# Unused products in the routing loop of the capacity experts, and at the end of the set-up

## The chip, the cores and the metric

The kernel runs on one core of one Trainium2 chip. The metric is the device time of one execution in microseconds (us), lower is better. Before the change the median of three runs is 2647.92 us (2641.19 to 2651.87).

## The reference

A chain of twelve stages works on `x` of 8 x 512 rows of 128 numbers. The stage that matters here is the feed-forward layer L0, which is used twice, as stage 0 and as stage 2, with the segment attention between them:

```python
x = x + 0.5 * L0_ffn(layernorm(x))      # stage 0
x = x + L0_attn(layernorm(x))           # stage 1
x = x + 0.5 * L0_ffn(layernorm(x))      # stage 2
...                                     # nine more stages

def L0_ffn(x):                          # 8 kinds: 7 experts and one that does nothing
    weights = softmax(x @ router_w.T + router_b)
    vals, idx = top_k(weights, 2)
    # each expert takes the first 512 of the 4096 rows that chose it
    h = relu(inputs[e] @ experts_inter[e])
    out[e] = (h @ experts_out[e]) * weight
    # every row gets back what its experts made of it;
    # the idle kind gives the row itself times its weight
```

## The kernel before, in words

`x` stays in SBUF for the whole kernel, as 32 tiles of 128 rows; four tiles make a block, so there are eight blocks (B = 8, TB = 4). Each stage is a block of instruction streams, one for each engine, tied by semaphores and written out by hand; a barrier of all engines (`clear`) stands between two stages. There is no planner: an engine does its list in the order in which it is written.

**The unused products.** `stir` (L174 to L178) issues n TensorE products of the 128x128 identity in bf16 with itself, repeated to 512 columns, into a PSUM bank whose content nobody reads. The kernel calls it in many places.

**The set-up** (`setup`, L181) loads x and the weights and prepares a few matrices. TensorE does almost nothing in it: two small products for the router and the gate (L249, L252), then, when VectorE has summed the eight adapters (L301, L303), one transpose (L315). VectorE then goes on with the signatures and the last copy (L311), and the barrier follows.

**The routing loop** is the first part of `capacity_experts_ffn` (L776). On TensorE, for b in 0 to 8: `turn_batch(b)` transposes the four tiles of x of block b (L867) into one of two banks in turn; then come two unused products (L919, shown under the line of the helper, L178); then `route(b - 1)` multiplies the turned block b - 1 by the router's eight columns (L874). `turn_batch(b)` waits until ScalarE has copied block b - 2 out of PSUM; `route(b)` waits for the copy of block b. ScalarE copies each turned block (L1094, `copy_xnT`) and, from the third copy on, normalises the four tiles of block b - 2 (L1087). VectorE takes the statistics of the eight blocks (L133, L138, L141), and GpSimd makes the deviations from them (L1139 to L1142). SyncE meanwhile clears two rows of results in HBM (L848).

When all eight blocks are routed, VectorE alone chooses the experts (`choose`, L963 to L977), TensorE counts (L924, L925), sixteen more unused products run, and the rows of each expert are found (`find_slots`, L885), gathered by indirect DMA (L1151), multiplied (L903, L912) and scattered (L1162). The next stage reads them back.

Of the kernel before, what the change touches and what calls it, by code (L numbers as in the profile page):

```python
# [61 lines left out]
def semaphores(nc, names):  # L62

    names = names.split()
    while len(ALL_SEMS.free) < len(names):
        ALL_SEMS.made += 1
        ALL_SEMS.free.append(ALL_SEMS.ctx.enter_context(nc.semaphore(f"stage{ALL_SEMS.made}")))
    taken, ALL_SEMS.free = ALL_SEMS.free[:len(names)], ALL_SEMS.free[len(names):]
    return namedtuple("Semaphores", names)(*taken)  # L70
# [11 lines left out]
def clear(nc, s, last=False):  # L82

    numbers = [h.num for h in s]
    assert not set(numbers) & {h.num for h in ALL_SEMS.free}
    assert min(numbers) > max([h.num for h in ALL_SEMS.lasting], default=-1)
    if last:
        numbers += [h.num for h in ALL_SEMS.lasting]
    nc.all_engine_barrier(sems_to_clear=range(min(numbers), max(numbers) + 1))  # L90
    ALL_SEMS.free = sorted([*s, *ALL_SEMS.free], key=lambda h: h.num)
# [82 lines left out]
def stir(pe, G, bank, n):  # L174

    for _ in range(n):
        pe.matmul(bank, G.ident16[:], G.ident16[:].unsqueeze(1).to_broadcast([P, 4, P]), start=True, stop=True)  # L178

def setup(nc, ctx, inp):  # L181

    sb = lambda n, shape, dt=F32: ctx.enter_context(nc.sbuf_tensor(n, shape, dt))
    G = Shared()

    G.x, G.minus_half = sb("x", [P, NT + TB, D]), sb("minus_half", [P, TB])
    G.ident, G.ident16 = sb("ident", [P, P]), sb("ident16", [P, P], BF16)

    G.WcT, G.bcomb = sb("WcT", [D, D]), sb("bcomb", [P, D])  # L190
    G.M, G.gateT = sb("M", [D, KINDS, D]), sb("gateT", [D, KINDS])
    G.route = sb("route", [D, KINDS + NCT + COMP_H])
    G.table = sb("table", [NCT, T_ALL])
    G.knots, G.inv_temp, G.out_scale = sb("knots", [P, KINDS]), sb("inv_temp", [P, 1]), sb("out_scale", [P, 1])
    G.cb1, G.cw2, G.cb2 = sb("cb1", [COMP_H, 1]), sb("cw2", [COMP_H, 2]), sb("cb2", [P, 2])
    G.half_gamma, G.half_beta, G.desc = sb("half_gamma", [P, D]), sb("half_beta", [P, D]), sb("desc", [P, KINDS])
    with ExitStack() as own:
        s = semaphores(nc, "x_loaded cleared made router_psum router_copied gate_loaded gate_psum gate_copied")
        segment, load_segment, clear_blocks = segment_attention_prepare(nc, ctx, G, inp)
        router, load_router, make_upto, raw_router = capacity_experts_prepare(nc, ctx, own, G, inp)  # L200
        center = own.enter_context(nc.sbuf_tensor("center", [P, P], F32))
        psC = own.enter_context(nc.psum_tensor("psC", [P, 512], F32))
        spline, load_spline, make_order, make_signatures = spline_prepare(nc, own, G, inp)
        adapters, load_weights, load_biases, combine_adapters, turn_adapters, copy_adapters = adapters_prepare(nc, own, G, inp)
        raw_gate = own.enter_context(nc.sbuf_tensor("raw_gate", [D, KINDS], F32))
        with nc.Block() as block:
            @block.sync
            def _(sp):
                for q in range(4):
                    sp.dma_start(G.x[:, q * NT // 4:(q + 1) * NT // 4, :],  # L210
                                  inp["L0_attn_x"].rearrange("b (t p) d -> p (b t) d", p=P)[
                                      :, q * NT // 4:(q + 1) * NT // 4, :]).then_inc(s.x_loaded, 16)
                load_router(sp)
                sp.dma_start(raw_gate[:], inp["L3_ffn_gate_wT"]).then_inc(s.gate_loaded, 16)
                load_biases(sp)
                load_segment(sp)
                sp.wait_ge(s.x_loaded, 64)
                sp.wait_ge(router.router_loaded, 32)

            @block.scalar  # L220
            def _(act):
                load_weights(act)
                load_spline(act)
                act.wait_ge(s.gate_loaded, 16)
                act.wait_ge(segment.seg_loaded, 128)

            @block.gpsimd
            def _(pool):
                pool.memset(G.minus_half[:], -0.5).then_inc(s.cleared, 1)
                pool.memset(G.x[:, NT:, :], 0.0).then_inc(s.cleared, 1)  # L230
                pool.memset(G.ident[:], 0.0).then_inc(s.cleared, 1)
                pool.wait_ge(s.cleared, 3)
                pool.affine_select(out=G.ident[:], in_=G.ident[:], compare_op=ALU.not_equal, fill=1.0,
                                   base=0, pattern=[[-1, P]], channel_multiplier=1).then_inc(s.made, 1)
                pool.wait_ge(s.made, 1)
                pool.tensor_copy(G.ident16[:], G.ident[:]).then_inc(s.made, 1)
                pool.wait_ge(s.made, 2)

                pool.tensor_scalar(center[:], G.ident[:], -1.0 / D, None, ALU.add).then_inc(s.made, 1)
                pool.wait_ge(s.made, 3)  # L240
                make_upto(pool)
                clear_blocks(pool)
                make_order(pool)

            @block.tensor
            def _(pe):
                pe.wait_ge(s.made, 3)
                pe.wait_ge(router.router_loaded, 32)
                pe.matmul(psC[:, 0:KINDS], center[:], raw_router[:], start=True, stop=True).then_inc(s.router_psum, 1)  # L249
                pe.wait_ge(s.gate_loaded, 16)  # L250
                pe.wait_ge(s.router_copied, 1)
                pe.matmul(psC[:, 0:KINDS], center[:], raw_gate[:], start=True, stop=True).then_inc(s.gate_psum, 1)  # L252
                turn_adapters(pe)

            @block.vector
            def _(dve):
                dve.wait_ge(s.router_psum, 1)
                dve.tensor_copy(G.routerT[:], psC[:, 0:KINDS]).then_inc(s.router_copied, 1)
                dve.wait_ge(s.gate_psum, 1)
                dve.tensor_copy(G.gateT[:], psC[:, 0:KINDS]).then_inc(s.gate_copied, 1)  # L260
                combine_adapters(dve)
                make_signatures(dve)
                copy_adapters(dve)
        clear(nc, s + router + segment + spline + adapters)
    return G
# [510 lines left out]
def capacity_experts_ffn(nc, G, inp, tag, rest):  # L776
# [12 lines left out]
    with ExitStack() as ctx:  # L789
# [46 lines left out]
        slots_ps, xT_ps = [pb(f"slots{i}", [P, 512]) for i in range(2)], pb("xT", [D, CAP])  # L836
# [5 lines left out]
        with nc.Block() as block:  # L842
# [19 lines left out]
            def _(pe):  # L862
# [53 lines left out]
                for b in range(B + 1):  # L916
                    if b < B:
                        turn_batch(b)
                    stir(pe, G, slots_ps[0][:], 2)  # L919
                    if b:  # L920
                        route(b - 1)
                pe.wait_ge(s.masked, 1)
# [273 lines left out]
def segment_attention_prepare(nc, ctx, G, inp):  # L1196
    sb = lambda n, shape, dt=F32: ctx.enter_context(nc.sbuf_tensor(n, shape, dt))
    G.seg_w = {n: sb(f"seg_{n}", [D, D]) for n in ("wq", "wk", "wv", "wc")}
    G.seg_bq, G.seg_bk = sb("seg_bq", [D, 1]), sb("seg_bk", [D, 1])
    G.seg_bv, G.seg_bc = sb("seg_bv", [D, 1]), sb("seg_bc", [P, D])  # L1200
    G.seg_P = sb("seg_P", [P, SB, TB, P])
    s = semaphores(nc, "seg_loaded seg_cleared")

    def load(dma):
        for n, w in G.seg_w.items():
            dma.dma_start(w[:], inp[f"L0_attn_{n}T"]).then_inc(s.seg_loaded, 16)
        dma.dma_start(G.seg_bq[:], inp["L0_attn_bq"].rearrange("(d a) -> d a", a=1)).then_inc(s.seg_loaded, 16)
        dma.dma_start(G.seg_bk[:], inp["L0_attn_bk"].rearrange("(d a) -> d a", a=1)).then_inc(s.seg_loaded, 16)
        dma.dma_start(G.seg_bv[:], inp["L0_attn_bv"].rearrange("(d a) -> d a", a=1)).then_inc(s.seg_loaded, 16)
        dma.dma_start(G.seg_bc[:], row_layout(inp["L0_attn_bc"])).then_inc(s.seg_loaded, 16)  # L1210

    def make(pool):
        pool.memset(G.seg_P[:], 0.0).then_inc(s.seg_cleared, 1)
        pool.wait_ge(s.seg_cleared, 1)
    return s, load, make
# [2022 lines left out]
```

## Time and profile before

| | |
|---|---|
| three timed runs, us | 2641.19, 2647.92, 2651.87 |
| the profiled execution, us | 2653.97 |
| its span, first to last instruction, us | 2652.2 |
| mean granted TensorE clock over the span | 0.922 |
| busy share: TensorE, VectorE, ScalarE, GpSimd | 83%, 74%, 67%, 37% |
| instructions in the trace | 47713 |
| stage 0: starts, router's last result read | 34.66, 51.62 us |
| stage 2: starts, router's last result read | 261.2, 288.68 us |

### The profile page before, as it was taken

What the parts mean: (1) busy time and instruction counts of PE and PEld (TensorE: products, weight loads), DVE (VectorE), ACT (ScalarE), POOL (GpSimd) and SP (SyncE); (2) the same over time, 40 slices, a digit from 0 to 9 for tenths busy, and PEclk for the clock granted to TensorE, in tenths of its full rate; (3) what the DMA queues carried; (4) which work ended last, traced back from release to release, by engine and by line L of the source; (5) the groups of instructions that cost most, each with busy time, mean ns of one, the idle gap of its engine ahead of it and who ended that gap; (6) DMA issues with size and microseconds to landing.
All of it is one profiled execution on the core that took longest, in us unless ns stands there. A gap on an engine that the chain in (4) does not pass through costs nothing. (4 is left out here: it accounts for less than half of the span.)

```text
span 2652.2 us, 47713 instructions
## 1 busy us (share of the span) xinstructions
PE 2196.8 (83%) x15155; PEld 1125.9 (42%) x15155; DVE 1958.0 (74%) x5765; ACT 1788.1 (67%) x4541; POOL 988.2 (37%) x1512
## 2 busy tenths in 40 slices
PE   3768785748888888589999999997868888888888
PEld 2446463512222225434444444445334444444453
DVE  4547626759989967768777777776688888888766
ACT  2224223327777774568888878785479999999965
POOL 2643354345445413600000000005645555555437
PEclk8889586759999996799999999999979999999999
DMA  4420514022322310100000000000020111111001
GB/s 140 112 84 13 155 40 135 1 48 59 78 53 55 79 25 1 33 1 1 2 1 1 2 1 2 2 2 1 7 64 1 33 33 33 33 33 33 1 1 32
DMA packets 227640, 94.85 MB, mean 36 GB/s; under 512 B 175746, under 2 KB 215490, under 8 KB 227394
## 3 DMA queue, kind: packets, MB, share of 16 engines
q1 hardware_dynamic: 220864, 83.46, 12.6%
q0 software_dynamic: 3584, 7.58, 1.0%
q8 instruction: 125, 2.05, 0.3%
q10 hardware_dynamic: 2946, 0.77, 0.2%
q14 instruction: 121, 0.99, 0.1%
HBM read 30.66 MB, written 19.17 MB: 19 GB/s over the span
## 5 line engine op out<-in xcount | busy, mean ns | idle before, releaser
L2345 DVE TENSOR_REDUCE s_neg_max<-s_ps_a 128x1 f32<-128x512 f32 x1024 | 662.3, 684 | 141.7 <-PE s_ps_a L2151 129.2
L2613 ACT ACTIVATE s_pT<-s_ps_t 128x512 f32<-128x512 f32 x1024 | 646.1, 659 | 135.8 <-PE s_ps_t L2185 116.4
L2604 ACT ACTIVATE s_first<-s_ps_a,s_neg_max 128x512 f32<-128x512 f32 x512 | 412.0, 805 | 14.0 <-DVE s_neg_max L2345 13.7
L2531 POOL TENSOR_SCALAR s_first<-s_first,s_rec 128x512 f32<-128x512 f32 x384 | 301.6, 801 | 282.6 <-DVE s_rec L2351 282.5
L2197 PE MATMUL s_ps_t<-ident,s_first 128*128 128x128 f32 x2048 | 313.6, 284 | 64.2 <-ACT s_pT L2613 51.2
L2977 DVE CUSTOM_DVE_ANT_0 s_e<-s_ps_a,w_alibi 128x128 f32<-128x128 f32 (+3 forms) x512 | 225.9, 488 | 126.7 <-PE s_ps_a L2813 126.3
L2151 PE MATMUL s_ps_a<-s_lanesT 64*128 64x512 bf16 x1024 | 272.2, 398 | 36.8 <-DMA s_lanesT<-n_lanes 21.2
L2197 PEld LDWEIGHTS s_ps_t<-ident,s_first 128*128 128x128 f32 x2048 | 220.5, 141 | 160.9 <-ACT s_pT L2613 117.4
L2215 PE MATMUL s_ps_o<-s_pT,n_v_pad 128*32 128x512 f32 x2048 | 272.8, 606 | 12.2 <-ACT s_oT L2619 12.2
L3085 ACT ACTIVATE s_e<-s_e,s_neg_max 128x128 f32<-128x128 f32 (+3 forms) x512 | 282.1, 564 | 0.0
L3093 ACT ACTIVATE s_pT<-s_ps_t 128x384 f32<-128x384 f32 (+1 forms) x320 | 156.3, 532 | 115.5 <-PE s_ps_t L2840 88.8
L154 POOL TENSOR_TENSOR s_rstd<-s_ve,minus_half 128x4 f32<-128x4 f32 x24 | 24.7, 1030 | 502.2 <-DVE s_ve L141 501.5
L2185 PE MATMUL s_ps_t<-s_shiftedT,s_lanesT 64*128 64x512 bf16 x512 | 167.2, 385 | 41.1 <-DVE s_neg_max L2345 30.0
L2813 PE MATMUL s_ps_a<-s_k_side,s_q_side 64*128 64x128 f32 (+3 forms) x1024 | 187.1, 460 | 3.6 <-DVE s_neg_max L2977 1.4
L2991 DVE TENSOR_SCALAR s_e<-s_e,s_rec 128x128 f32<-128x128 f32 (+3 forms) x512 | 163.3, 383 | 4.5
L2604 ACT ACTIVATION_READ_ACCUMULATOR s_first<-s_ps_a,s_neg_max 128x1 f32 x512 | 166.2, 325 | 0.0
L2856 PE MATMUL s_ps_vo<-s_pT,s_v 128*64 128x512 f32 (+3 forms) x1024 | 163.3, 441 | 0.0
L2840 PEld LDWEIGHTS s_ps_t<-ident,s_e 64*128 64x128 f32 x2176 | 107.8, 140 | 89.6 <-issue 45.7
L2151 PEld LDWEIGHTS s_ps_a<-s_lanesT 64*128 64x128 bf16 x1024 | 62.1, 93 | 179.1 <-issue 106.3
L2185 PEld LDWEIGHTS s_ps_t<-s_shiftedT,s_lanesT 64*128 64x128 bf16 x512 | 38.5, 93 | 221.2 <-ACT s_pT L2613 160.0
L703 PE MATMUL s_ps_y<-M,s_xT 128*128 128x512 f32 x256 | 119.8, 612 | 10.3 <-DVE x L599 8.3
L2840 PE MATMUL s_ps_t<-ident,s_e 64*128 64x64 f32 x2176 | 115.1, 224 | 13.9 <-issue 4.5
(428 smaller groups left out, 4138.4 us busy)
## 6 DMA issues: line engine op xcount, KB each, us to landing
s_y_rows<-s_zeros SPq DMA_DIRECT2D x4, 2048.0 KB, 10.0
s_parts<-s_y_rows SPq DMA_DIRECT2D x32, 256.0 KB, 3.8
s_token_rows<-s_rows SPq DMA_DIRECT2D x2, 2176.0 KB, 10.3
s_Wi<-L_ffn_experts_inter SPq DMA_DIRECT2D x2, 1792.0 KB
x<-L_attn_x SPq DMA_DIRECT2D x4, 512.0 KB, 8.1
out<-x SPq DMA_DIRECT2D x8, 256.0 KB, 2.3
s_lanesT<-n_lanes SPq DMA_TRANSPOSE x64, 4.6
s_shiftedT<-n_lanes SPq DMA_TRANSPOSE x64, 2.4
```

The lines of the kernel that those rows point to most:

```text
L2151: pe.matmul(sa[n % NA][:], lanesT[rows_of(a), j % 2, 0, pair, t * P:(t + 1) * P], lanesT[rows_of(a), j % 2, 1, pair, :], start=True, stop= ...
L2185: pe.matmul(st[n % NK][:], lanesT[rows_of(a), j % 2, 1, pair, i * P:(i + 1) * P], shiftedT[rows_of(a), p % NS, :], start=True, stop=True). ...
L2197: last = pe.transpose(st[n % NK][:, t * P:(t + 1) * P], first[:, p % NF, 2 * t + a, i * P:(i + 1) * P], G.ident[:])
L2215: last = pe.matmul(o_ps[32 * c:32 * c + 32, :], G.v_pad[j % 2][:, (g % PB * TB + kt) * 2 + c % 2, :], pT[:, (PU * g + 2 * kt + c % 2) % NP ...
L2345: dve.tensor_reduce(neg_max[:, column(n):column(n) + 1], sa[n % NA][:], AX.X, ALU.max, negate=True).then_inc(s.max_ready, 1)
L2531: do.free(pool.tensor_scalar(f, f, rec1[:, n:n + 1], 1.0, ALU.mult, ALU.mult))
L2604: act.activation(first[:, g % NF, n % PU, :], sa[n % NA][:], ACT.Exp, bias=neg_max[:, n:n + 1], accum_out=sum1[:, n % (NR * PU):n % (NR * ...
L2613: act.activation(pT[:, n % NP, :], st[n % NK][:], ACT.Exp).then_inc(s.probs_ready, 1)
L2813: pe.matmul(sa[t % 2][a][:, 0:width(t)], q_side[g % NS][rows, t * P:(t + 1) * P], k_side[g % NS][rows, 0:width(t)], start=True, stop=True) ...
L2840: last = pe.transpose(turn_bank(m, half)[:, first + t * HALF_P:first + (t + 1) * HALF_P], e[rows, g % NF, 2 * t + a, kt * P:(kt + 1) * P], ...
L2977: dve.tensor_tensor_reduce(e[:, g % NF, 2 * t + a, 0:width(t)], sa[t % 2][a][:, 0:width(t)], G.alibi[:, h, (TB - 1 - t) * P:L], -1.0, 3e38 ...
L3085: act.activation(part, part, ACT.Exp, bias=neg_max[:, n:n + 1], scale=-1.0, accum_out=total[:, n:n + 1]).then_inc(s.first_ready, 1)
```

## The change

Two edits. In the routing loop the two unused products stay for blocks 2 to 8 and become five after blocks 0 and 1; the loop runs in stage 0 and in stage 2. At the end of the set-up's TensorE stream ten unused products are added, into the bank psC, whose last content VectorE has taken by then. The wait ahead of them is for the bf16 identity, which GpSimd made at the start of the set-up.

```diff
@@ setup, TensorE
                 pe.matmul(psC[:, 0:KINDS], center[:], raw_gate[:], start=True, stop=True).then_inc(s.gate_psum, 1)
                 turn_adapters(pe)
+                pe.wait_ge(s.made, 2)
+                stir(pe, G, psC[:], 10)
 
@@ capacity_experts_ffn, TensorE
                 for b in range(B + 1):
                     if b < B:
                         turn_batch(b)
-                    stir(pe, G, slots_ps[0][:], 2)
+
+                    stir(pe, G, slots_ps[0][:], 2 if b > 1 else 5)
                     if b:
                         route(b - 1)
```

That is 10 + 2 x 6 = 22 more products of 512 columns, none of which is read.

## Rows read from the trace of the kernel before

**Rows 1.** The page: granted clock in 40 slices of 66.3 us, in tenths.

```profile
PEclk8889586759999996799999999999979999999999
```

**Rows 2.** Busy time by stretch: routing loop of stage 0, its rest, the same of stage 2.

```profile
34.66:51.62 16.96, 16.35 (x114) 13.76 (x114) 10.78 (x73) 14.33 (x33) 13.49 (x32) 1.00 0.67 249
51.62:163.18 111.56, 77.20 (x564) 50.97 (x564) 56.79 (x176) 24.37 (x45) 58.29 (x55) 0.84 0.32 89
261.20:288.68 27.48, 27.37 (x114) 23.40 (x114) 10.75 (x73) 15.51 (x36) 13.48 (x32) 0.50 0.44 164
288.68:405.44 116.76, 83.24 (x564) 53.97 (x564) 56.91 (x176) 21.89 (x40) 58.38 (x55) 0.79 0.30 83
```

**Rows 3.** Order of time, routing loop of stage 0 (start, duration, engine).

```profile
34.66 1.09 PE L867 MATMUL s_ps_xT<-ident,x 128*128 128x128 f32 x4 [5.32 <-PEq L90]
...
35.54 1.06 PE L178 MATMUL s_ps_slots<-ident 128*128 128x512 bf16 x2
...
39.05 0.64 PE L867 MATMUL s_ps_xT<-ident,x 128*128 128x128 f32 x4
...
39.53 0.59 PE L178 MATMUL s_ps_slots<-ident 128*128 128x512 bf16 x2
39.73 0.60 ACT L1094 ACTIVATE s_xnT<-s_ps_xT 128x512 f32<-128x512 f32 x1 [1.64 <-PE s_ps_xT L867]
...
39.96 0.95 PE L874 MATMUL s_ps_up<-routerT,s_xnT 128*128 128x8 f32 x8
...
40.77 0.63 PE L867 MATMUL s_ps_out<-ident,x 128*128 128x128 f32 x4
...
51.62 0.42 DVE L963 TENSOR_TENSOR s_logits<-s_ps_up,s_rstd 128x256 f32<-128x256 f32 x1 [5.64 <-PE s_ps_up L874]
```

**Rows 4.** Order of time, routing loop of stage 2.

```profile
262.10 1.06 PE L178 MATMUL s_ps_slots<-ident 128*128 128x512 bf16 x2
...
262.95 1.06 PE L867 MATMUL s_ps_out<-ident,x 128*128 128x128 f32 x4
...
264.65 1.72 PE L874 MATMUL s_ps_up<-routerT,s_xnT 128*128 128x8 f32 x8
...
266.22 1.09 PE L867 MATMUL s_ps_xT<-ident,x 128*128 128x128 f32 x4
...
269.53 1.09 PE L867 MATMUL s_ps_out<-ident,x 128*128 128x128 f32 x4
...
288.68 0.42 DVE L963 TENSOR_TENSOR s_logits<-s_ps_up,s_rstd 128x256 f32<-128x256 f32 x1 [16.17 <-PE s_ps_up L874]
```

**Rows 5.** Waits in 261:289 (who for whom, us in total, times, longest).

```profile
DVE s_logits L963 <- PE s_ps_up L874: 16.2, 1, 16.2
ACT s_xnT L1094 <- PE s_ps_xT L867: 15.8, 4, 10.7
```

**Rows 6.** Order of time, last part of the set-up.

```profile
28.86 0.48 PE L315 MATMUL psW<-ident,Wsum 128*128 128x128 f32 x1 [12.86 <-DVEq L305]
...
33.48 0.29 DVE L311 TENSOR_SCALAR WcT<-psW 128x128 f32<-128x128 f32 x1
```

**Rows 7.** Granted clock by stretch around the ends of work (columns as in rows 2).

```profile
52.00:56.00 4.00, 0.00 (x0) 0.00 (x0) 3.28 (x9) 3.41 (x9) 0.00 (x0) 0.51 0.15 48
...
255.00:260.00 5.00, 3.23 (x18) 2.71 (x17) 1.61 (x3) 0.00 (x0) 0.00 (x0) 0.82 0.00 0
260.00:265.00 5.00, 3.79 (x15) 2.86 (x15) 3.69 (x24) 1.20 (x2) 2.46 (x5) 0.53 0.42 150
```

**Rows 8.** By stretch after the loop: to the first gather; first to last scatter; both stages.

```profile
51.62:76.35 24.73, 10.12 (x88) 5.15 (x88) 20.93 (x58) 3.79 (x10) 0.00 (x0) 0.65 0.62 178
...
103.03:163.18 60.15, 46.94 (x315) 33.83 (x313) 17.58 (x61) 15.61 (x27) 39.11 (x39) 0.96 0.15 43
288.68:313.32 24.64, 11.01 (x88) 5.33 (x88) 20.88 (x57) 1.95 (x5) 0.00 (x0) 0.64 0.59 164
...
340.19:405.44 65.25, 50.69 (x308) 36.04 (x304) 17.50 (x61) 14.97 (x27) 39.01 (x39) 0.88 0.14 40
```

## The prediction

> **What bounds the kernel now.** I read the page's clock row first: the granted TensorE clock is near full almost everywhere, but the slice from 265 to 331 us shows 5 tenths, and that is where stage 2 begins [rows 1]. Then the busy times by stretch, with both routing loops cut out. The same 114 products take 16.96 us in stage 0 and 27.48 us in stage 2, at a granted clock of 0.50 in the second [rows 2]. So the two loops, which are one piece of code, differ by 10.5 us, and the reader is to see that the slow one is TensorE's: it is busy 27.37 of 27.48 us, and the longest waits there are VectorE's for the last router product (16.2 us) and ScalarE's for a turned block (15.8 us in four waits) [rows 5].
>
> The order of time gives each loop's pace. In stage 2 block 2 is turned at 266.22 and block 3 at 269.53: 3.31 us a block, all of it TensorE at 1.2 GHz [rows 4]. In stage 0 the unused products at 35.54 take 1.06 us a pair, those at 39.53 only 0.59: the clock rose between, after four unused products and eight transposes (the clock column shows 1.00 for the whole loop [rows 2], but the durations before 38.4 are those of 1.2 GHz, so I go by the durations) [rows 3]. From then on TensorE needs 40.77 - 39.05 = 1.72 us a block [rows 3], and ScalarE sets the pace: from its copy of block 2 at 39.73 to the last router product read at 51.62 are 11.89 us [rows 3], six blocks at about 2.0. That tail is what a loop costs once its clock is up; with the clock down it is 21 us. Nothing else covers these microseconds: `choose`, which starts when the loop ends, is VectorE alone, and 24.73 and 24.64 us pass from there to the first gather in the two stages [rows 8]. So what the loop of stage 2 wins moves on into the stage.
>
> **The change, part by part.** Prices in a row of products, from starts. At 1.2 GHz: an unused pair 262.95 - 262.10 = 0.85, so 0.425 for one; a block's router products 266.22 - 264.65 = 1.57; its transposes 3.31 - 0.85 - 1.57 = 0.89 [rows 4]. At 2.4 GHz: transposes 0.48, pair 0.43 (0.215 for one), router products 0.81 [rows 3].
>
> (1) Stage 2's loop. The first product follows the first transposes at 262.10, as before. Five at 1.2 GHz end at 262.10 + 2.13 = 264.23, the transposes of block 1 at 265.1, five more at 267.2. Up to there TensorE has streamed 128 or 512 columns without a pause, against one pair in 3.3 us before. In stage 0 the rise came after 3.7 us of a thinner mix [rows 3], so I take the clock as up when the ten are through, 267.2. Then router products of block 0 (0.81), transposes of block 2 from 268.0, ScalarE's copy 0.68 later as in stage 0 (39.05 to 39.73 [rows 3]), at 268.7, and 11.89 more: 280.6 instead of 288.68, **-8.1**. Bounds: were the clock up at 264.9, 3.7 us after the loop's start, the second five end at 266.2 and the loop at 279.6 (-9.1); if it rises one block later, the router products of block 0 and the transposes of block 2 still cost 1.57 and 0.89: 281.5 or so (-7.2).
>
> That it then stays up I read from stage 0: the same six blocks with two products each run at 1.00 until the loop is over, and the clock is down at 52 us [rows 2, 7]. The Trainium skill speaks against that: "TensorE: Matmul & The Clock Gate", section Part 4: PE-mode transpose, holds that transposes do not count as work for the full clock. By it the two products of a later block stand nearly alone and the clock falls again: term (1) would be about 0 instead of -8.1, which is rival C. The loop of stage 0, half of whose streamed columns are transposes, does not bear it out.
>
> (2) Stage 0's loop. It was up early already. If the clock starts low as before: 34.66, first five from 35.54 to 37.67, transposes to 38.5, where it rose before; the second five at 0.215 to 39.6, router 40.4, copy of block 2 at 41.1 against 39.73: **+1.4**. If the set-up's products leave it up from the first transpose: 34.66 + 0.48 + 1.08 + 0.48 + 1.08 + 0.81 + 0.68 = 39.3: -0.5. I take +1.4, since the clock did fall around the short pause before stage 2: 0.82 in 255:260, 0.53 in 260:265 [rows 7], and the set-up also ends in a pause of about 1 us.
>
> (3) The ten products of the set-up. They start after the transpose, near 29.3, and need 4.27 us at 1.2 GHz: to 33.6. VectorE's last copy ends at 33.77, and the loop starts at 34.66, TensorE having waited 5.32 us [rows 3, 6]. So VectorE's chain hides them: **0**. Without that cover they would be 4.3; as it is 0.1 at most, if the barrier sees their end a little after VectorE's. Nothing queues behind them on TensorE but the barrier; no engine waits for psC.
>
> (4) What follows. The first scatter to the last takes 60.15 us at a clock of 0.96 in stage 0 and 65.25 at 0.88 in stage 2 [rows 8]: the same work, 5.1 apart by where the clock happened to fall. Moving stage 2 by 8 us deals these cards anew. I put 0 in the sum and 5 each way in the range.
>
> Sum against the execution profiled (2653.97 us, of which the span is 2652.2): -8.1 + 1.4 + 0 = -6.7, so 2647.3. That execution lies 6.05 above the median of the runs. The spread of all four, 12.8 us, is about what one loop costs at the low clock (10.5), so some of the runs may have had it up. Taking the whole -6.7 off the median gives 2641.2, taking the median's lower time for a partly warm loop gives 2647.3; I choose the middle, **2644 us**, -0.15%.
>
> **Rivals.**
> (A) The forecast: stage 2's loop goes from 27.5 to about 19.4 us, and most of it is seen in the median. 0.56.
> (B) The median execution already had both loops up, and only the profiled one was unlucky. Then each loop pays the six products, 1.4 each: 2650.7, slower by 0.1%. For it: 2641.19 among the timed runs. Against it: 2647.92 and 2651.87, as well as the profile, are on the high side. It decides as soon as the loop of stage 2 rises by itself within its first two blocks. 0.20.
> (C) The clock rises for the ten products and falls back in the later blocks. Price: six products of 0.425 (2.55) are paid and one or two blocks at 1.72 instead of 3.31 are won (1.6 to 3.2), so about 0 in stage 2, with +1.4 in stage 0: 2647.9 + 1.4 = 2649.3. Stage 0's 1.00 [rows 2] speaks against it. This is the case that the rule on transposes in the Trainium skill's "TensorE: Matmul & The Clock Gate" would bring about. 0.07.
> (D) The clock doesn't rise at all, and the change is only six products longer, 2.55 in each loop: 2653. TensorE rose for thinner work in stage 0. 0.04.
> (E) The median execution had both loops down; then both win, 8.1 and 27.48 - (16.96 + 1.4) = 9.1: 2630.7. The spread allows it, the only profile has stage 0 up. 0.08.
> (F) The clock in the experts' part or further on falls badly: five or more on top of B, 2656 to 2662. 0.05.
>
> **How the numbers follow.** The likeliest is A, 2644. Its own range is 2639 to 2649 (the bounds of 1 and 2 give -9.6 to -5.8, the experts' part 5 each way, partly cancelling). To hold 8 in 10 the range takes in B and C above and half of the way to E below: 2636 to 2653. What a measurement of this kernel can tell from no change is about 0.5%, 13 us: faster than that needs under 2634.7, which is E; slower needs over 2661.2, the end of F. Faster 0.08, same 0.89, slower 0.03.
>
> **What would show it.** Right: the ten unused products after the first two transposes of stage 2 start at durations of 0.63 and end at 0.38; the granted clock of the loop's later blocks is 1.00; the loop from first transpose to L963 lasts 18 to 20 us; ScalarE's waits for turned blocks shrink to the first two; the stretch from L963 to the first gather stays 24.7. Stage 0's loop lasts 16.5 to 18.4 us and begins no later than before, at 34.7. Wrong: durations of 0.63 still at block 3 of stage 2 (C, D), a loop of stage 0 that starts at 35 or later (3), or a gain in the loop that the stretch between the scatters gives back (4, F). The forecast of the time is wrong, though each step be right, if the runs before differ by whether their loops were warm, since one profile cannot tell how often.

## The result, and the profile after

The changed kernel takes 2631.23 us in the median of 20 runs (2629.86 to 2637.11). The kernel before, run beside it 20 times, takes 2643.43 us (2624.47 to 2663.37). The ratio is 0.9952, with a 95% interval of 0.9935 to 0.9969: faster by half a per cent, 12.2 us between the medians. The forecast was 2644, with a range of 2636 to 2653. The time lies below the range, and it is next to rival E (2630.7, with a chance of 0.08). What also changed is the spread: 39 us before, 7 us after. In the means of the runs the kernels are 11.8 us apart (2643.96 and 2632.13). The change also gives something up: the two best runs of before, 2624.47 and 2625.00, lie 5 us below the best run of the changed kernel.

The busy times by stretch of the changed kernel, as in [rows 2] (TensorE, its weight loads, VectorE, ScalarE, GpSimd, then the granted clock):

```profile
34.45:50.94 16.49, 15.83 (x120) 13.14 (x120) 10.81 (x74) 14.38 (x33) 13.23 (x31) 1.00 0.69 256
50.94:157.50 106.56, 75.41 (x564) 50.47 (x564) 56.80 (x176) 24.52 (x45) 58.92 (x58) 0.86 0.33 93
255.90:275.20 19.30, 18.66 (x120) 14.50 (x120) 10.74 (x74) 13.10 (x32) 13.44 (x32) 0.85 0.64 232
275.20:382.70 107.50, 78.24 (x564) 51.79 (x564) 56.85 (x176) 24.56 (x45) 58.35 (x55) 0.80 0.32 90
```

Stage 2's loop went from 27.48 to 19.30 us, stage 0's from 16.96 to 16.49. The rests of the two stages went from 111.56 and 116.76 to 106.56 and 107.50. The two profiled spans are 21.0 us apart (2652.2 and 2631.2): 8.7 from the loops, 14.3 from the rests, and about 2 us given back in later stages. So the pair of profiles alone would say that the gain is mostly in the experts' part. The experiments below say otherwise. Besides, the profile of before was taken ahead of the prediction and that of the change behind it, and whether both come from one chip is not on record.

The order of time of TensorE in stage 2's loop, the answer to [rows 4] (the line numbers have moved by 2 or 3, L869 is the transposes, L876 the router's products):

```profile
255.92 1.09 PE L869 MATMUL s_ps_xT<-ident,x 128*128 128x128 f32 x4 [1.87 <-PEq L90]
256.80 2.34 PE L178 MATMUL s_ps_slots<-ident 128*128 128x512 bf16 x5
258.93 1.06 PE L869 MATMUL s_ps_out<-ident,x 128*128 128x128 f32 x4
259.78 2.19 PE L178 MATMUL s_ps_slots<-ident 128*128 128x512 bf16 x5
261.81 0.95 PE L876 MATMUL s_ps_up<-routerT,s_xnT 128*128 128x8 f32 x8
262.62 0.64 PE L869 MATMUL s_ps_xT<-ident,x 128*128 128x128 f32 x4
263.09 0.59 PE L178 MATMUL s_ps_slots<-ident 128*128 128x512 bf16 x2
...
264.33 0.64 PE L869 MATMUL s_ps_out<-ident,x 128*128 128x128 f32 x4
```

Nearly all of the ten products run at 1.2 GHz. The router's products behind them take 0.95 us where they took 1.72, and a block costs 264.33 - 262.62 = 1.71 us. From there ScalarE sets the pace, at 2.0 us a block, without a pause:

```profile
263.29 0.60 ACT L1097 ACTIVATE s_xnT<-s_ps_xT 128x512 f32<-128x512 f32 x1 [2.67 <-PE s_ps_xT L869]
263.79 1.64 ACT L1090 ACTIVATE s_rows<-x,s_minus,s_rstd 128x128 f32<-128x128 f32 x4
265.32 0.58 ACT L1097 ACTIVATE s_xnT<-s_ps_out 128x512 f32<-128x512 f32 x1
```

ScalarE's waits for turned blocks and VectorE's for the last router product have shrunk against [rows 5], where ScalarE's waits for the other of the two banks were, before the change:

```profile
ACT s_xnT L1094 <- PE s_ps_out L867: 4.6, 4, 1.2
```

and after it:

```profile
ACT s_xnT L1097 <- PE s_ps_xT L869: 13.3, 2, 10.6
DVE s_logits L966 <- PE s_ps_up L876: 8.0, 1, 8.0
...
ACT s_xnT L1097 <- PE s_ps_out L869: 2.4, 1, 2.4
```

Over both banks ScalarE's waits went from 20.4 us (eight waits) to 15.7 us (three), and most of what is left, 10.6 us, is the wait for the stage's first block. VectorE's went from 16.2 to 8.0 us.

In the set-up and at the start of stage 0, the answer to [rows 3, 6]:

```profile
32.38 0.91 PE L178 MATMUL psC<-ident 128*128 128x512 bf16 x2
...
33.32 0.29 DVE L313 TENSOR_SCALAR WcT<-psW 128x128 f32<-128x128 f32 x1
...
34.45 0.63 PE L869 MATMUL s_ps_xT<-ident,x 128*128 128x128 f32 x4 [1.17 <-PEq L90]
```

The ten products end at 33.3, ahead of VectorE's last copy, and the loop starts at 34.45 (34.66 before). The first transposes already take 0.63 us, not 1.09: the clock survived the pause of 1.17 us.

### The profile page after: what moved, and what is told of

It is laid out like the page before. It is cut to its first block and busy times, and to the rows that moved or that the text cites. A ratio compares the mean times of both kernels' runs of the same rounds, so it can differ in the third digit from the quotient of the medians.

```text
span 2631.2 us, 47757 instructions
## 1 busy us (share of the span) xinstructions
PE 2187.5 (83%) x15177; PEld 1116.2 (42%) x15177; DVE 1956.4 (74%) x5765; ACT 1787.4 (68%) x4541; POOL 986.4 (37%) x1512
## 3 DMA queue, kind: packets, MB, share of 16 engines
q1 hardware_dynamic: 220864, 83.46, 12.8%
## 5 line engine op out<-in xcount | busy, mean ns | idle before, releaser
L2218 PE MATMUL s_ps_o<-s_pT,n_v_pad 128*32 128x512 f32 x2048 | 272.8, 606 | 12.2 <-ACT s_oT L2622 12.2
L3088 ACT ACTIVATE s_e<-s_e,s_neg_max 128x128 f32<-128x128 f32 (+3 forms) x512 | 281.8, 563 | 0.0
L2843 PE MATMUL s_ps_t<-ident,s_e 64*128 64x64 f32 x2176 | 115.2, 224 | 13.9 <-issue 4.5
## 6 DMA issues: line engine op xcount, KB each, us to landing
s_Wi<-L_ffn_experts_inter SPq DMA_DIRECT2D x2, 1792.0 KB, 16.2
```

What stands on the lines that cost most here:

```text
L2218: last = pe.matmul(o_ps[32 * c:32 * c + 32, :], G.v_pad[j % 2][:, (g % PB * TB + kt) * 2 + c % 2, :], pT[:, (PU * g + 2 * kt + c % 2) % NP ...
L2843: last = pe.transpose(turn_bank(m, half)[:, first + t * HALF_P:first + (t + 1) * HALF_P], e[rows, g % NF, 2 * t + a, kt * P:(kt + 1) * P], ...
L3088: act.activation(part, part, ACT.Exp, bias=neg_max[:, n:n + 1], scale=-1.0, accum_out=total[:, n:n + 1]).then_inc(s.first_ready, 1)
```

## The experiments

Four theories stand against each other. L: the gain is that each loop is sure of the 2.4 GHz clock, which before it got or missed by chance. S: the set-up's ten products carry it. E: the experts' part gets quicker whenever its loop was quick. P: the experts' part depends on how long before the loop's end the clock last changed, and the change happens to fix a good distance.

The kernels of one session ran on one chip, with the kernel before between them, and each session had a chip of its own. The level differs from session to session (medians of the kernel before: 2649.45, 2664.91 and 2660.93 us in the three with timed rounds), so times are compared inside a session only. The ratio is formed on its own and comes out nearer to 1 than that of the medians; I give both.

**One part at a time.**

```diff
 a1_loop_only:    stir(pe, G, slots_ps[0][:], 2 if b > 1 else 5)      # nothing in the set-up
 a2_setup_only:   stir(pe, G, psC[:], 10)                             # loops as before
 a3_second_only:  stir(pe, G, slots_ps[0][:], 5 if b < 2 and tag == "s2" else 2)
 a4_before_again: the kernel before
```

a1_loop_only. 

> Five products after blocks 0 and 1 in both loops, nothing in the set-up. Theory L (the gain is that each loop is sure of the 2.4 GHz clock, and what follows is chance): stage 2's loop 18 to 20 us, stage 0's loop about 18.3 us (1.4 over its best), the whole 1 to 2 us above the full change, so a ratio to before near 0.996. Theory S (the set-up's ten products carry the gain, because they start stage 0 at 2.4 GHz and everything behind falls well): ratio near 1.000, with stage 2's loop shorter all the same. Theory E (the experts' part gets quicker whenever its loop was at 2.4 GHz): the stretch from first gather to last scatter is near 82 us in both stages, as in the changed kernel, and not 87 to 92.

a2_setup_only. 

> Ten products at the end of the set-up, two everywhere in the loops. Theory L: stage 0's loop is sure of 2.4 GHz from its first product and takes about 15.2 us (16.5 of the changed kernel less six products of 0.215), stage 2's is left to chance (17 to 27.5 us); ratio near 0.998, runs spread by more than 10 us. Theory S: ratio near 0.995 as with the full change and runs within 7 us. Theory E: the experts' part of stage 0 near 82 us, that of stage 2 short only if its loop was at 2.4 GHz.

a3_second_only. 

> Five products after blocks 0 and 1 in stage 2's loop alone. Theory L: stage 2's loop 18 to 20 us, stage 0's 17 to 27.5 us by chance; ratio near 0.998, spread between that of before and that of the change. Theory S: ratio near 1.000. Theory E: stage 2's stretch from first gather to last scatter near 83 us, stage 0's 82 to 88.

a4_before_again. 

> The kernel before once more, for a second profile of it. All theories: ratio 1.000. Theory L says that the two loops take 17 us or 27.5 us whichever way the clock falls, and that this alone spreads the runs by about 10 to 20 us. Theory E says that the experts' part takes 82 us behind a loop that had 2.4 GHz and 87 to 92 behind one that had 1.2 GHz; the first profile has 86.8 behind a loop at 2.4 GHz, which speaks against it.

Measured, the kernel before at 2649.45 us (35 runs, 2624.48 to 2670.09), twelve runs each. The columns "loop" are of the one profiled execution.

| | median, us | ratio (95%) | loop 0 | loop 2 | rest 0 | rest 2 |
|---|---|---|---|---|---|---|
| a1 loops only | 2635.45 | 0.9975 (0.9942 to 1.0008) | 18.66 | 19.09 | 106.0 | 107.3 |
| a2 set-up only | 2647.34 | 0.9983 (0.9941 to 1.0025) | 15.42 | 17.26 | 106.0 | 106.0 |
| a3 stage 2 only | 2641.15 | 0.9985 (0.9954 to 1.0017) | 27.51 | 18.68 | 106.4 | 106.7 |
| a4 before again | 2650.08 | 1.002 (0.9981 to 1.0059) | 17.18 | 27.51 | 110.8 | 106.3 |

All four intervals hold 1, so no part can be told from none by its ratio; the profiles and the groups of runs say more. So do the means, which suit runs that fall into groups better than the median: against a mean of 2647.43 us before, a1 is 9.0 us lower (standard error 2.7), a2 7.0 (4.3) and a3 5.4 (2.4), while a4, the same kernel, is 2.0 higher. That fits a gain in each of the two loops, but the errors are too large to share it out. Stage 0's loop of a3, code of before, took 27.51 us at 1.2 GHz:

```profile
34.49:62.00 27.51, 27.37 (x114) 23.41 (x114) 10.78 (x74) 16.79 (x37) 13.53 (x32) 1.00 0.45 164
```

(The clock column reads 1.00 there only because no change of clock is on record before; the duration is that of [rows 2]'s second loop.) In a2 stage 0's loop started on the set-up's clock in the one profile, and stage 2's is left alone: four of the twelve runs lie at 2623.1 to 2624.5 us, the other eight at 2638.5 to 2654.8, and the profiled one, of the first group, had a loop of 17.26 us in stage 2. An old loop therefore goes either way. If the two groups are its two ways, which the runs without a profile do not show, it went well here in a third of them. Theory S wanted the whole gain and runs within 7 us in a2: they spread over 32 us. Its ratio alone does not decide, since the interval holds both 0.995 and 1. And a1 gains without the set-up's products. Theory E, in the form that the rest is quicker behind a quick loop, falls too: behind the loops of 27.51 us the rests are 106.4 and 106.3.

**Nine stages in a row.** To see more loops in one profile, I ran chains of stages, which leave out most of the reference.

```diff
-ALL = ("ffn0", "attn0", "ffn0", "ffn1", "attn1", "ffn1", "ffn2", "attn2", "ffn2", "ffn3", "attn3", "ffn3")
+ALL = ("ffn0", "attn0") * 8 + ("ffn0", "ffn1", "ffn3")
 c3 besides:      stir(pe, G, slots_ps[0][:], 2 if b > 1 else 5)
 c3, d3, d7, ahead of the first use of the router's products, n = stage number, 3 or 7:
+                    for _ in range(n):
+                        do(dve.tensor_reduce(m[:], te(logits_ps), AX.X, ALU.max))
 d7 besides, behind them, twice:
+                    do(dve.memset(ones_r[:], 1.0))
```

c1_nine_old. 

> Leaves out most of the reference: nine times the capacity experts with the segment attention behind each (the spline layer behind the ninth), then the linear experts; two products in every block, as in the kernel before. One profile gives nine routing loops and nine experts' parts. Loops: all theories say a mixture of about 17 and 27.5 us. Theory P (place): the rest of the stage, from the loop's last result to the last scatter, depends on how long before that result the clock last changed, whatever the change does; so it is spread over 106 to 117 us here, with several above 110. Theory E (the rest is quicker behind a quick loop): 106 behind loops of 17 us, 111 or more behind loops of 27.5 us.

c3_nine_shift. 

> The same nine stages, with five products after blocks 0 and 1, and VectorE does n extra reductions of 0.46 us each, whose result is written over, ahead of the first use of the router's products, n = 0 in the first stage to 8 in the ninth (0 to 3.7 us). Loops of 18 to 19.5 us in all theories. Theory P: the rest, counted from the first real use, is 106 to 108 for n = 0, 110 to 117 for some n near 2 or 3 (the loop's result is then used 14.6 to 15.3 us after the rise, where one profile has 116.8), and 106 to 108 again for n = 8. Theory E and chance: no dependence on n.

The nine routing loops of c1, one profile:

```profile
33.30:60.80 27.50, 27.36 (x114) 23.38 (x114) 10.75 (x73) 16.78 (x37) 13.48 (x32) 1.00 0.45 164
278.00:305.51 27.51, 27.37 (x114) 23.40 (x114) 10.73 (x74) 15.50 (x36) 13.47 (x32) 0.50 0.45 163
518.43:535.74 17.31, 16.66 (x114) 14.10 (x114) 10.73 (x73) 13.09 (x32) 13.47 (x32) 0.87 0.68 250
750.57:767.86 17.29, 16.64 (x114) 14.09 (x114) 10.73 (x73) 13.09 (x32) 13.47 (x32) 0.87 0.68 249
984.58:1012.08 27.50, 27.36 (x114) 23.38 (x114) 10.73 (x74) 15.50 (x36) 13.47 (x32) 0.50 0.45 164
...
1941.68:1969.18 27.50, 27.37 (x114) 23.41 (x114) 10.73 (x73) 15.50 (x36) 13.47 (x32) 0.50 0.45 164
```

Two loops at 17.3, seven at 27.5, nothing between. c3's nine loops take 17.85 to 22.25 us, and less their own delay of 0.46 us a reduction 17.9 to 19.4: the five products bring the clock up nine times out of nine. The whole executions, one run each on the same chip, take 2303.42 us (c1) and 2263.54 us (c3): 39.9 us apart, where the loops in sum, delays included, are 42.4 us apart.

The rests are 113.1 to 119.1 us in c1 (mean 115.3) and 113.1 to 119.2 in c3 (mean 115.2). In c3, for n = 0 to 8, they are 113.1, 114.8, 116.3, 119.2, 115.8, 113.3, 115.0, 114.8 and 114.4. The top at n = 3 and the return at 8 look like theory P's curve, but its numbers (106 to 108 at both ends) did not come, and one stage for each n, in a range that c1 shows without any delay, does not show it. What the two chains do show is that the rest has the same mean behind old and new loops. The full kernels with delays:

d3_shift3. 

> The whole changed kernel with three such reductions ahead of the first use in both loops, 1.4 us each, 2.7 us in sum. Theory P: the experts' parts get slower as well, 5 to 20 us more in sum, so 2639 to 2654 in the median. Theory E and chance: the 2.7 us alone, 2634.

d7_shift7. 

> The same with seven reductions and two short fills, 3.4 us in each loop, 6.8 us in sum, more than the kernel with three has. Theory P: the place is again as without any, so the 6.8 us alone: 2638, at or below the kernel with three. Theory E and chance: 2638, that is 4 us above the kernel with three.

The kernel before took 2664.91 us in that session, d3 2654.16 (ratio 0.9981, 0.9954 to 1.0007) and d7 2668.54 (1.002, 0.999 to 1.0049). The absolute numbers expected do not fit, since the chip was slower as a whole (d3 came out at the upper end of P's range, d7 31 us above its). Theory P wanted d7 at or below d3; it came 14.4 us above it, where the delays alone differ by 4. But this is not a clean test of P. Of the 14.6 us between their two profiled spans, 11.9 lie in the last 815 to 825 us, and nearly all of that is one loop. The linear experts of the last stage route their rows by the same mix of products as the loop here: four transposes, two unused products, eight records of gate products a block. The change leaves that loop alone. In d7 it ran like this:

```profile
2565.71 0.63 PE L686 MATMUL s_ps_xT<-ident,x 128*128 128x128 f32 x4 [2.51 <-PEq L90]
2566.17 0.66 PE L178 MATMUL s_ps_y<-ident 128*128 128x512 bf16 x2
2566.62 1.06 PE L686 MATMUL s_ps_y<-ident,x 128*128 128x128 f32 x4
...
2569.89 1.09 PE L686 MATMUL s_ps_xT<-ident,x 128*128 128x128 f32 x4
...
2573.20 1.09 PE L686 MATMUL s_ps_y<-ident,x 128*128 128x128 f32 x4
```

From its first transpose to the end of its last gate product it took 26.55 us, at 3.31 us a block to the end. In the ten other profiles of the full kernel that stretch takes 15.7 to 15.9 us. So the third loop of this kind draws too, if more rarely, and here the clock fell from 2.4 to 1.2 GHz after the first few products and did not come back. In the first profile of the changed kernel it fell at the same place (first transposes 0.63 us, second 1.06) and was back at the third (0.63). What stays against theory P are the rests, which are alike in d3 (115.7 and 113.4 us) and d7 (114.9 and 113.3).

The profile of d3 shows one thing more. Behind the set-up's ten products its loop of stage 0 still began at 1.2 GHz:

```profile
34.16 1.09 PE L869 MATMUL s_ps_xT<-ident,x 128*128 128x128 f32 x4 [1.02 <-PEq L90]
```

In the six other profiles of kernels with these ten products the first transposes take 0.63 us. So the set-up's products alone do not make stage 0 sure; in d3 it was the five products in the loop that brought the clock up.

**The change again, the clock brought up ahead, and no products at all.**

```diff
 e2_ahead_both: set-up as in the change, loops with 2 products, and in segment_attention
+                    if j == B:
+                        stir(pe, G, q_ps[0][:], 2)
                     if j >= 1:
                         output(j - 1)
+                    if j == B:
+                        stir(pe, G, q_ps[0][:], 3)
                     if j + 1 < B:
                         project(j + 1)
+                    if j == B - 1:
+                        stir(pe, G, q_ps[1][:], 10)
 e3_none_in_loop: before, with
-                    stir(pe, G, slots_ps[0][:], 2)
+                    stir(pe, G, slots_ps[0][:], 0)
```

e1_after_again. 

> The changed kernel itself, for a second profile and for its time beside before on the same chip. Theory L (what the change brings is that both loops are sure of the 2.4 GHz clock; before, a loop had it in about one execution of three: 5 of the 15 old loops profiled so far): loops of 16.5 to 19.5 us, a median 10 to 13 us below before on this chip, whatever the absolute level. Theory E (the gain is in the experts' part): that part, 106 to 107 us in the first profile of it, is again 5 to 9 us shorter than before's. Chance: the median difference is that of stage 2's loop alone, 7 us or less.

e2_ahead_both. 

> Two products in every block of both loops as before, ten at the end of the set-up, and fifteen in the pauses of TensorE at the end of the segment attention (ten before the last small transpose, two before and three after the last output), so that stage 2 also begins at 2.4 GHz. Theory L: both loops of 15.4 to 17.3 us with nothing paid in them, a median 3 to 5 us below the changed kernel on the same chip, runs within 10 us. Theory E: no better than the changed kernel. If the clock falls in the pause at the barrier and does not come back: stage 2's loop 27.5 us in a part of the runs, median 5 us or more above the changed kernel.

e3_none_in_loop. 

> No unused product in the loops, none in the set-up. If unused products are only worth what the clock gives back, the loop stays at 1.2 GHz but each block costs 3.31 - 0.85 = 2.46 us: two loops of about 20.5 us, 41 us in sum, against 36 for the change and 48 in the mean for before: a median 7 us below before and 5 above the change. If the clock rises all the same, 17 us a loop, as quick as the change or quicker. If the transposes count for nothing and the clock never rises, 20.5 in every profile.

| | median, us | ratio (95%) | loop 0 | loop 2 | rest 0 | rest 2 |
|---|---|---|---|---|---|---|
| before | 2660.93 (27 runs) | 1 | | | | |
| e1 the change | 2645.78 | 0.9946 (0.9917 to 0.9974) | 16.47 | 18.61 | 109.6 | 114.5 |
| e2 ahead of both | 2642.34 (10 runs) | 0.9926 (0.9893 to 0.996) | 15.43 | 15.18 | 114.4 | 116.5 |
| e3 none | 2646.94 | 0.995 (0.9919 to 0.9981) | 20.36 | 20.21 | 112.9 | 112.7 |

The change is 15.2 us below before on this chip, though its experts' parts take 109.6 and 114.5 us, and not the 106 to 107 of its first profile. So the gain comes again without theory E's 106. How long the experts' part of the kernel before takes on this chip is not known, since it was not profiled there; theory E is out by a3 and a4, not by this run. e3's loop stays at 1.2 GHz from end to end:

```profile
265.94:286.15 20.21, 20.07 (x96) 19.77 (x96) 10.73 (x73) 15.11 (x36) 13.46 (x32) 0.50 0.61 223
```

and its blocks cost 2.46 us (transposes at 37.18 and 39.64), as expected:

```profile
37.18 1.09 PE L867 MATMUL s_ps_xT<-ident,x 128*128 128x128 f32 x4
38.07 1.72 PE L874 MATMUL s_ps_up<-routerT,s_xnT 128*128 128x8 f32 x8
39.64 1.09 PE L867 MATMUL s_ps_out<-ident,x 128*128 128x128 f32 x4
```

Its median is 1.2 us above the change's, where 5 were expected. Leaving the products out wins as much against before as adding more of them, inside what can be told (in the means 12 and 15 us, with standard errors of about 3). e2 has the shortest loops and the lowest median, 3.4 us under the change, but its interval overlaps the change's.

g1_nine_ahead is the chain of nine stages with e2's edits. 

> The nine capacity stages again (most of the reference left out), two products in every block as in the old chain, with ten products at the end of the set-up and fifteen at the end of each segment attention. Theory L: the clock is up at or soon after the start of each loop, nine loops of 15 to 17.5 us where the old chain had two of 17.3 and seven of 27.5; the execution 8 to 10 us a loop shorter in its loops, so 2303 - 65 to 80 = 2223 to 2238 if the rest is the same. If the pause at the barrier loses the clock in some phases: a part of the nine at 27.5. The rest of each stage 113 to 119 on a chip like that of the old chain, 106 to 112 on one like the first.

```profile
33.61:49.03 15.42, 14.77 (x114) 12.50 (x114) 10.75 (x73) 14.26 (x33) 12.24 (x25) 1.00 0.74 274
261.10:276.28 15.18, 14.53 (x114) 12.58 (x114) 10.74 (x73) 13.09 (x32) 12.00 (x25) 1.00 0.75 278
...
1831.11:1846.29 15.18, 14.53 (x114) 12.57 (x114) 10.74 (x74) 13.09 (x32) 12.01 (x25) 1.00 0.75 278
```

Nine loops of 15.17 to 15.42 us: the set-up's ten products have the first loop at 2.4 GHz from its first transpose, and fifteen products in the pauses of the stage ahead have the other eight. The execution took 2177.60 us, 125.8 less than c1's: 90.3 in the loops (227.1 against 136.9 us in sum), the rest in experts' parts of 109.7 to 114.8 us and in shorter attentions. It ran in a session of its own, so only the 90.3 can be told from the level of the chip.

## Why the prediction was wrong, step by step

**What bounds the loop** was right: at 1.2 GHz TensorE, 3.31 us a block, at 2.4 GHz ScalarE, 2.0. That the clock is near full almost everywhere was misread: the slices of [rows 1] show 6, 7 and 5 tenths again between 398 and 597 us.

**(1) Stage 2's loop** was right for the execution that it was worked out for: 8.1 us forecast, 8.18 measured (27.48 to 19.30), and 8.9 in the change's second profile (18.61). The clock rose at the end of the ten products and stayed up. The rule of the Trainium skill ("TensorE: Matmul & The Clock Gate", section Part 4: PE-mode transpose), by which transposes do not count as work for the full clock, would have had it fall back in the later blocks; it did not, so rival C is out for this loop. The rule itself is not settled by that, since every later block also holds two products of 512 columns. That e3's loop, with transposes and no products of 512 columns, never rose does agree with it. And something like rival C did happen once, in the last stage's loop of d7. Two slips in the working: of the columns that a block streams (4 x 128 in transposes, 2 x 512 in unused products, 8 x 8 in router products) the transposes are a third, not half, and if the clock rises a block later, ScalarE's copy comes 1.13 us behind the transposes, as at 266.22 in [rows 4], and the loop ends at 281.8, a win of 6.9 us and not 7.2.

**(2) Stage 0's loop: the step that failed.** I wrote "It was up early already" and booked +1.4. That was true of the one execution profiled. Of the 15 loops with the old code that I have in profiles (two in before, two in a4, one in a2, one in a3, nine in c1), five took 17.0 to 17.3 us and ten 27.5. Stage 0's own loop, with nothing added ahead of it, is in four of them: 16.96 us in before, 17.18 in a4, 27.51 in a3 and 27.50 in c1, in the mean 22.3. Stage 2's is in four as well (27.48, 27.51, 17.26 in a2, 27.51 in c1), in the mean 24.9. The change brings them to 16.5 and to 19.0. So stage 0, where I had booked a loss of 1.4 us, wins 5.8, about as much as stage 2 with 6.0. Together that is 11.4 to 12.1 us by the change's two profiles (pairs of 35.8 and 35.1 against 47.2), where the means of the runs differ by 11.8 and the medians by 12.2. Over all 15 loops the mean is 24.1 and the win 12.4 to 13.1. That these figures meet is partly luck: four draws a place are few, and how the win is shared between the two loops is argued from them, not shown. The +1.4 itself was mis-sized as well: the set-up's products do leave the clock up (first transposes 0.63 us, in six profiles of seven), and the loop took 0.47 us less even against a good one, my lower bound of -0.5.

**The step from the execution to the median** failed with it. I took the runs' spread of 12.8 us as a sign that the median run had a part of the gain already, and shrank the gain from 6.7 to 3.9 us. The last sentence of the prediction names the condition that came true, that the runs before differ by whether their loops were up, but the chances gave it next to nothing. Where one loop of two in a profile is slow and the code is the same, the forecast should have been over draws. If the draws were independent, and the 15 loops a fair sample, both would be good in about 1 execution of 9, one of them in 4 of 9, none in 4 of 9. Neither was tested.

Part of the miss is no step of the argument: the median of before was 2647.92 us in three runs and 2643.43 in twenty. Of the 12.8 us between forecast and result 4.5 are this, and 8.3 the gain, 12.2 instead of 3.9. Rival E is near for the same reason: it priced a gain of 17.2 us, 5 too much, from a start 4.5 too high. Its time was right by luck, though its case, both loops down, is one that a3's and c1's first loops do not rule out.

**(3) The set-up's products at 0** was right: they end at 33.3, VectorE's copy at 33.6, the stage starts no later.

**(4) The experts' part, 0 with 5 each way**, was too narrow for a pair of profiles (14.3 us between these two), but right in the mean: 115.3 us behind old loops and 115.2 behind new ones in the chains. That the two stages differ "by where the clock happened to fall" is not borne out: a rest of 106.4 us had a mean granted clock of 0.93 (a3, stage 0) and one of 107.3 had 0.80 (a1, stage 2), while one of 112.9 had 0.90 (e3, stage 0).

**Rivals.** D (the clock never rises) is out by the profiles, and B (the median execution had both loops up) by the result, since B has the change slower. F did not come.

**Open.** The runs of before spread over 39 us and over 46 in the next session, more than the 21 of two loops. In a2 the upper group begins 14 us above the lower and reaches 31, where one loop is worth 10. So a further cost goes with some executions. One such cost is the last stage's loop, 10.7 us in d7; whether it was slow in a2's upper group or in the slow runs of before is not known, as those runs have no profile. Theory P, my attempt at it, found no support. Why the changed kernel's 20 runs lay within 7 us in the first comparison and its 12 runs within 23 (2634.79 to 2657.65) on the later chip is open too.

## What to carry to other kernels

A stretch whose pace hangs on TensorE's clock can be a lottery: the same code took 17.3 or 27.5 us. Look at every place where the same mix of products runs, and at the spread of the runs, before taking one profile as the kernel. Here the change mended two such places and left those of the linear experts. Unused products pay if they have the clock up before the stretch begins, in a pause that is hidden anyway (loops of 15.2 to 15.4 us in the twelve profiled with two products a block that began so), but it can fall again or not have risen yet, as the loops of d7's last stage and d3's stage 0 show. Inside the stretch they cost 0.43 us each as long as the clock stays down: eighteen of them in an undecided loop gave 24.1 us in the mean, and none gave 20.3. A change that makes a stretch certain wins the bad draws and pays for it in the good ones, so its gain is a mean over draws, and no single profile shows it.

## What the runs showed of the hardware that I had not expected

A TensorE that is busy 27.37 of 27.51 us by the trace can stay at 1.2 GHz all along, seven times of nine in c1, and in the same code rise in the other two. It can also start such a loop at 2.4 GHz and fall back: in d7's last stage TensorE had waited 2.51 us, and the clock fell within a microsecond of the loop's start, while after waits of 1.17 to 1.23 us (the changed kernel's stage 0, e2's stage 2) the clock stayed up.

The experts' part shows pauses of TensorE in the middle of a group of products that wait for nothing on record. In stage 2 of the kernel before:

```profile
357.58 2.01 PE L912 MATMUL s_ps_out<-s_Wo,s_hidden 128*128 128x128 f32 x14
359.83 0.27 PE L912 MATMUL s_ps_out<-s_Wo,s_hidden 128*128 128x128 f32 x1 [0.24 <-issue]
360.55 0.36 PE L912 MATMUL s_ps_out<-s_Wo,s_hidden 128*128 128x128 f32 x1 [0.45 <-issue]
361.26 0.27 PE L912 MATMUL s_ps_out<-s_Wo,s_hidden 128*128 128x128 f32 x1 [0.35 <-issue]
362.65 3.47 PE L912 MATMUL s_ps_out<-s_Wo,s_hidden 128*128 128x128 f32 x15 [1.13 <-issue]
```

and in the second profile of the changed kernel, on the later chip, in another group:

```profile
338.46 0.64 PE L887 MATMUL s_ps_slots<-s_told,s_one_hot 128*32 128x32 bf16 x19
339.64 0.25 PE L887 MATMUL s_ps_slots<-s_told,s_one_hot 128*32 128x32 bf16 x4 [0.54 <-issue]
340.36 0.18 PE L887 MATMUL s_ps_slots<-s_told,s_one_hot 128*32 128x32 bf16 x1 [0.47 <-issue]
341.07 0.35 PE L887 MATMUL s_ps_slots<-s_told,s_one_hot 128*32 128x32 bf16 x8 [0.54 <-issue]
```

In these lines the starts that follow a pause are 0.71 or 0.72 us apart, once 1.39. The first profile of the changed kernel and the four profiles of the first session have no such pause over 0.2 us in their experts' parts, and their rests are 106 to 107.5 us but for one of 110.8. Every experts' part with such pauses has a rest of 109.6 us or more. The pauses go with the slow rests; what makes them was not tested, and since each session used its own chip, chip and cause cannot be told apart here.
